# Eight-core attention and block FFN kernel: the float32 to bf16 casts of half of the FFN's second weight move from GpSimd to ScalarE

## The chip, the cores and the metric

The kernel runs on the eight cores of one Trainium2 chip. Each core takes one of the eight batch entries (2048 tokens of 2048 features) and computes its whole output; all weights go to every core, and the cores exchange nothing. The metric is the device time of the slowest core, in microseconds (us). "Before" and "after" are timed as medians of several runs.

## What is computed

The reference, cut to what matters (x is 8 x 2048 x 2048, float32):

```python
xn = layernorm(x)
# attention without a softmax, 16 heads of 128
q, k, v, u = xn @ Wq, xn @ Wk, xn @ Wv, xn @ Wu
q = relu(q) / sqrt(128); k = relu(k) / sqrt(128); u = silu(u)
kv = einsum('bhlk,bhlv->bhkv', k, v)
s  = (rms_norm(einsum('bhlk,bhkv->bhlv', q, kv)) * u) @ Wo
# FFN in 16 blocks of 512 hidden features; each token keeps its 4 best blocks
mask = top4(softmax(xn @ Wr.T + br))          # tokens x 16
h = gelu(xn @ W1.T) * mask                    # tokens x 8192, a mask value per block
g = silu(h @ W2.T)                            # W2.T is 8192 x 2048
out = x + s * g
```

## The kernel before

Five engines each run an instruction list of their own, in order: TensorE (PE), VectorE (DVE), ScalarE (ACT), GpSimd (POOL) and SyncE (SP). They meet only at semaphores that count upward. cT, cV, cS and cG count the finished operations of PE, DVE, ACT and POOL. dS0 to dS3 and dG0 to dG3 count the transfers issued by SP and by POOL, four semaphores each in turn. The helper `dma` makes its engine wait until the transfer issued four before it on the same family has landed. The order of each list is the order in which the Python code appends to it; nothing reorders it afterwards. A wait holds everything behind it on its engine.

The work goes through stages: layer norm, transposes and the router (to about 611 us in the profile), K, V and their product (to 1394 us), the FFN (to 4967 us), then Q, U and attention by head (to 6662 us), and last the output projection with Wo (L621 to L665).

The change is in the FFN. It is done for two halves of 1024 tokens (`Hh`), and in each half for 8 slabs of 1024 hidden features (`slab`), so 16 slabs in all. One slab is:

- Mask rows: four small DMAs `mrow` (L396), four small matmuls (L398), and two casts to `mbc` by ACT (L402).
- GEMM 1, eight steps `jc`: SP loads two halves of a W1 tile (`w1ring`, L411), ACT casts them to bf16 (`w1b`, L414), PE does 32 matmuls of 128x512 into `hps` (L423), ACT applies gelu into `hm` (L427), DVE multiplies by the mask (L431).
- GEMM 2, twice, for the output halves `fh` = 0 and 1 of 1024 features each. First 16 tiles of W2 (128 x 512 float32, 256 KB) are loaded (L445) and cast into the bf16 buffer `w2b[fh]`. Only when all 16 have been cast does PE start 128 matmuls into `yps` (L463), 16 for each of 8 token tiles, and DVE adds each result to `y_acc` in SBUF (L472, or copies it in the first slab, L470).

The 16 W2 tiles pass through `w2ring`, two float32 buffers that both halves share. For `fh` = 0 SP issues the transfers and ACT casts (L450). For `fh` = 1 POOL issues them and POOL itself casts (L453). `w2cast_slot` and `w2cast_slot_g` hold the semaphore values of the last cast by ACT and by POOL from each buffer; the issuing engine waits for both before it overwrites the buffer. The first half's matmuls of PE (from `w2b[0]`) and the second half's loads (into `w2b[1]`) can run side by side.

The same form of ring appears once more, in the output projection: two buffers `woring`, loads by POOL (L633), casts by ACT (L637), 16 tiles of 128 x 512 float32, and PE starts (L651) when all have been cast.

Of the kernel before, what the change touches and what calls it, by code (L numbers as in the profile page):

```python
# [92 lines left out]
def build(nc):  # L93
    es = ExitStack()
    p = Prog(nc, es)
# [21 lines left out]
    cT = p.sem("cT")  # L117
    cV = p.sem("cV")
    cS = p.sem("cS")
    cG = p.sem("cG")  # L120
# [172 lines left out]
    for ncx in range(4):  # L293
        par = ncx % 2
        for i in range(NC):
            rs = (ncx * NC + i) % 4
            p.w("sync", cS, wring_cast[rs])
            dd = p.dma("sync", lambda e, i=i, ncx=ncx, rs=rs: e.dma_start(out=wring[rs][:], in_=wk_d[i * 128:(i + 1) * 128, ncx * 512:(ncx + 1) * 512]), dS)
# [5 lines left out]
        for i in range(NC):  # L304
            rs = (ncx * NC + i) % 4
            p.w("sync", cS, wring_cast[rs])
            dd = p.dma("sync", lambda e, i=i, ncx=ncx, rs=rs: e.dma_start(out=wring[rs][:], in_=wv_d[i * 128:(i + 1) * 128, ncx * 512:(ncx + 1) * 512]), dS)
# [51 lines left out]
    w2b = [p3.enter_context(nc.sbuf_tensor(f"w2b{i}", [128, 8 * 1024], BF16)) for i in range(2)]  # L359
# [14 lines left out]
    w2cast_slot = [0, 0]  # L374
    w2cast_slot_g = [0, 0]
    w2cons_fh = [0, 0]
# [5 lines left out]
    for Hh in range(2):  # L382
        tok0 = Hh * 1024
        for slab in range(8):
            b0 = slab * 2
            if (Hh, slab) != (0, 0):
                p.w("tensor", cS, gelu_done[(Hh, slab - 1, 7) if slab > 0 else (Hh - 1, 7, 7)])
            p.w("tensor", cS, mask_done[NT - 1])
            for bb in range(2):
                b = b0 + bb  # L390
                if bb == 1:
                    p.w("tensor", cS, p.v(cS))
                for gg in range(2):
                    p.w("sync", cS, mask_done[NT - 1])
                    p.w("sync", cT, mrow_guard[0])
                    mrow_dma = p.dma("sync", lambda e, b=b, gg=gg, tok0=tok0: e.dma_start(out=mrow[0:1, :], in_=maskT[b:b + 1, tok0 + gg * 512: tok0 + (gg + 1) * 512]), dS)  # L396
                    p.wd("tensor", mrow_dma)
                    p.e("tensor", lambda e, gg=gg: e.matmul(hps[0][:, gg * 512:(gg + 1) * 512], onesrb[0:1, :], mrow[0:1, :], start=True, stop=True), inc=cT)  # L398
                    mrow_guard[0] = p.v(cT)
                bcmm = p.v(cT)  # L400
                p.w("scalar", cT, bcmm)
                p.e("scalar", lambda e, bb=bb: e.copy(out=mbc[bb][:], in_=hps[0][:, 0:1024]), inc=cS)  # L402
            mbc_done = p.v(cS)
            p.w("tensor", cS, mbc_done)

            for jc in range(8):
                jg = slab * 8 + jc
                sl = jc % 2
                for hf in range(2):
                    p.w("sync", cS, w1cast[hf])  # L410
                    w1dma[hf] = p.dma("sync", lambda e, jg=jg, hf=hf: e.dma_start(out=w1ring[hf][:], in_=w1r_d[jg, :, hf * 1024:(hf + 1) * 1024]), dS)  # L411
                    p.wd("scalar", w1dma[hf])
                    p.w("scalar", cT, w1cons[hf])
                    p.e("scalar", lambda e, hf=hf: e.copy(out=w1b[hf][:], in_=w1ring[hf][:]), inc=cS)  # L414
                    w1cast[hf] = p.v(cS)
                if (Hh * 64 + jg) >= 1:
                    p.w("tensor", cS, gelu_done.get((Hh, slab, jc - 2), gelu_done.get((Hh, slab - 1, jc + 6), 0)))
                for hf in range(2):
                    p.w("tensor", cS, w1cast[hf])
                    for ng in range(2):  # L420
                        for ii in range(8):
                            i = hf * 8 + ii
                            p.e("tensor", lambda e, i=i, ii=ii, ng=ng, sl=sl, hf=hf, tok0=tok0: e.matmul(hps[sl][:, ng * 512:(ng + 1) * 512], w1b[hf][:, ii * 128:(ii + 1) * 128], A[:, i * L + tok0 + ng * 512: i * L + tok0 + (ng + 1) * 512], start=(i == 0), stop=(i == NC - 1)), inc=(cT if (i == NC - 1 and ng == 1) or (ii == 7 and ng == 1) else None))  # L423
                    w1cons[hf] = p.v(cT)
                hmm = p.v(cT)
                p.w("scalar", cT, hmm)
                p.e("scalar", lambda e, jc=jc, sl=sl: e.activation(out=hm[:, jc * 1024:(jc + 1) * 1024], in_=hps[sl][:], func=AF.Gelu), inc=cS)  # L427
                gelu_done[(Hh, slab, jc)] = p.v(cS)
                p.w("vector", cS, gelu_done[(Hh, slab, jc)])
                p.w("vector", cS, mbc_done)  # L430
                p.e("vector", lambda e, jc=jc, bb=jc // 4: e.tensor_tensor(out=hm[:, jc * 1024:(jc + 1) * 1024], in0=hm[:, jc * 1024:(jc + 1) * 1024], in1=mbc[bb][:], op=OP.mult), inc=cV)  # L431
                hmmask_done[(Hh, slab, jc)] = p.v(cV)
            hm_ready = p.v(cV)

            for fh in range(2):
                qeng = "sync" if fh == 0 else "gpsimd"
                qsem = dS if fh == 0 else dG
                ceng = "scalar" if fh == 0 else "gpsimd"
                csem = cS if fh == 0 else cG
                for jc in range(8):  # L440
                    jg = slab * 8 + jc
                    for cc in range(2):
                        p.w(qeng, cS, w2cast_slot[cc])
                        p.w(qeng, cG, w2cast_slot_g[cc])
                        dd = p.dma(qeng, lambda e, jg=jg, fh=fh, cc=cc: e.dma_start(out=w2ring[cc][:], in_=w2t_d[jg * 128:(jg + 1) * 128, fh * 1024 + cc * 512: fh * 1024 + (cc + 1) * 512]), qsem)  # L445
                        p.wd(ceng, dd)
                        if jc == 0 and cc == 0:
                            p.w(ceng, cT, w2cons_fh[fh])
                        if fh == 0:
                            p.e("scalar", lambda e, jc=jc, fh=fh, cc=cc: e.copy(out=w2b[fh][:, jc * 1024 + cc * 512: jc * 1024 + (cc + 1) * 512], in_=w2ring[cc][:]), inc=cS)  # L450
                            w2cast_slot[cc] = p.v(cS)
                        else:
                            p.e("gpsimd", lambda e, jc=jc, fh=fh, cc=cc: e.tensor_copy(w2b[fh][:, jc * 1024 + cc * 512: jc * 1024 + (cc + 1) * 512], w2ring[cc][:]), inc=cG)  # L453
                            w2cast_slot_g[cc] = p.v(cG)
                w2_ready = p.v(csem)
                p.w("tensor", cV, hm_ready)
                p.w("tensor", csem, w2_ready)
                for t8 in range(8):
                    sl = t8 % 2
                    p.w("tensor", cV, yadd_slot[sl])  # L460
                    for jc in range(8):
                        for fg in range(2):
                            p.e("tensor", lambda e, t8=t8, jc=jc, fg=fg, fh=fh, sl=sl: e.matmul(yps[sl][:, fg * 512:(fg + 1) * 512], hm[:, jc * 1024 + t8 * 128: jc * 1024 + (t8 + 1) * 128], w2b[fh][:, jc * 1024 + fg * 512: jc * 1024 + (fg + 1) * 512], start=(jc == 0), stop=(jc == 7)), inc=(cT if (jc == 7 and fg == 1) else None))  # L463
                    ymm = p.v(cT)
                    p.w("vector", cT, ymm)
                    if slab == 0:
                        if Hh == 1:
                            p.w("vector", cS, silu_mark)
                            p.dbar("vector", dG)
                        p.e("vector", lambda e, t8=t8, fh=fh, sl=sl: e.tensor_copy(y_acc[:, t8 * D + fh * 1024: t8 * D + (fh + 1) * 1024], yps[sl][:]), inc=cV)  # L470
                    else:
                        p.e("vector", lambda e, t8=t8, fh=fh, sl=sl: e.tensor_tensor(out=y_acc[:, t8 * D + fh * 1024: t8 * D + (fh + 1) * 1024], in0=y_acc[:, t8 * D + fh * 1024: t8 * D + (fh + 1) * 1024], in1=yps[sl][:], op=OP.add), inc=cV)  # L472
                    yadd_slot[sl] = p.v(cV)
                w2cons_fh[fh] = p.v(cT)
        yfin = p.v(cV)
        for t8 in range(8):
            p.w("scalar", cV, yfin)
            p.e("scalar", lambda e, t8=t8: e.activation(out=y_acc[:, t8 * D:(t8 + 1) * D], in_=y_acc[:, t8 * D:(t8 + 1) * D], func=AF.Silu), inc=cS)
            gdone = p.v(cS)
            p.w("gpsimd", cS, gdone)  # L480
            gst_dma[0] = p.dma("gpsimd", lambda e, t8=t8, tok0=tok0: e.dma_start(out=g_d[tok0 + t8 * 128: tok0 + (t8 + 1) * 128, :], in_=y_acc[:, t8 * D:(t8 + 1) * D]), dG)
        silu_mark = p.v(cS)
# [258 lines left out]
```

How the kernel before makes its waits and increments, by code:

```python
    def dma(self, eng, fn, q):  # L51
        i = self.val[q + "_i"] % self.NSL
        self.val[q + "_i"] += 1
        sub = f"{q}{i}"
        self.w(eng, sub, self.val[sub])
        self.val[sub] += 16
        h = self.sems[sub]
        self.st[eng].append(lambda e, fn=fn, h=h: fn(e).then_inc(h, 16))
        return (sub, self.val[sub])
# [12 lines left out]
    def w(self, eng, sem, v=None):  # L72
        vv = self.val[sem] if v is None else v
        h = self.sems[sem]
        self.st[eng].append(lambda e, h=h, vv=vv: e.wait_ge(h, vv))
# [1 line left out]
    def e(self, eng, fn, inc=None, k=1, dma=False):  # L77
        if not dma and eng in self.SELF:
            own = self.SELF[eng]
            self.w(eng, own, self.val[own])
            inc, k = own, 1
        if inc is not None:
            h = self.sems[inc]
            self.val[inc] += k
            self.st[eng].append(lambda e, fn=fn, h=h, k=k: fn(e).then_inc(h, k))
        else:
            self.st[eng].append(lambda e, fn=fn: fn(e))
```

## Time and profile before

| what | value |
|---|---|
| three timed runs | 7519.0, 7566.81 and 7606.86 us, median 7566.81 |
| the profiled execution | 7322.0 us |
| its slowest core, number 2: first to last instruction | 7320.1 us |
| its other cores | 7207.8 to 7307.4 us |
| PE busy in the span | 3723.1 us, 51% |
| ACT and DVE busy | 1186.6 us (16%) and 1146.8 us (16%) |
| POOL busy | 638.4 us (9%) |
| mean granted TensorE clock, core 2 | 0.766 |

The profiled execution is one execution of the program under the hardware profiler, and its rows are those of its slowest core where no other is named. Times inside it count from the first instruction. PEld is PE's loading of weights, which runs beside the matmuls. The names SPq and POOLq mark transfers that these engines issue, which are not counted as busy time of the engine; in the timeline a row of a transfer shows how long its issue took. The granted clock is a share of TensorE's full speed: 0.50 is 1.2 GHz and 1.00 is 2.4 GHz.

### The profile page before, as it was taken

What the parts mean: (1) busy time and instruction counts of PE and PEld (TensorE: products, weight loads), DVE (VectorE), ACT (ScalarE), POOL (GpSimd) and SP (SyncE); (2) the same over time, 40 slices, a digit from 0 to 9 for tenths busy, and PEclk for the clock granted to TensorE, in tenths of its full rate; (3) what the DMA queues carried; (4) which work ended last, traced back from release to release, by engine and by line L of the source; (5) the groups of instructions that cost most, each with busy time, mean ns of one, the idle gap of its engine ahead of it and who ended that gap; (6) DMA issues with size and microseconds to landing.
All of it is one profiled execution on the core that took longest, in us unless ns stands there. A gap on an engine that the chain in (4) does not pass through costs nothing.

```text
span 7320.1 us, 49442 instructions; the slowest of 8 cores (7207.8 to 7320.1 us)
## 1 busy us (share of the span) xinstructions
PE 3723.1 (51%) x15250; PEld 1514.3 (21%) x15250; DVE 1146.8 (16%) x1750; ACT 1186.6 (16%) x1667; POOL 638.4 (9%) x1003
## 2 busy tenths in 40 slices
PE   2224777855656555655556565555434443443444
PEld 1112322322222222222222222222111111111111
DVE  3331000010101110101101011101222222222000
ACT  2222111111221111221112111112111111110000
POOL 0000000011000111001110011110000000001222
PEclk9999777777878777877778787777656666666777
DMA  1001111122222222232232222222000000002333
GB/s 42 29 24 52 46 46 41 35 69 81 84 79 71 73 73 81 84 108 74 69 81 83 78 72 70 68 90 69 23 23 12 23 23 23 14 20 60 105 101 102
DMA packets 154608, 439.67 MB, mean 60 GB/s; under 512 B 23232, under 2 KB 23232, under 8 KB 150256
## 3 DMA queue, kind: packets, MB, share of 16 engines
q1 hardware_dynamic: 103424, 251.77, 11.5%
q0 software_dynamic: 50928, 184.75, 8.7%
q8 instruction: 128, 2.10, 0.1%
q14 instruction: 128, 1.05, 0.1%
HBM read 402.82 MB, written 33.55 MB: 60 GB/s over the span
## 4 chain that ended last, share of the span: by engine, by line
PE 40%; DMA 29%; ACT 10%; DVE 9%; issue 8%; POOL 4%; ACTq 0%; DVEq 0%; POOLq 0%; SPq 0%
DMA w2ring<-w2t 17%; PE hps L423 14%; PE yps L463 6%; DMA gst<-gscr 4%; PE kp L322 4%; PE qp L538 4%; PE vp L327 3%; PE qp L547 3%; DVE srow L592 3%; POOL w2b L453 2%; ACT w1b L414 2%; ACT hm L427 2%; PE bcp L597 2%; DMA woring<-wo 2%; DMA wring<-wqr 2%
## 5 line engine op out<-in xcount | busy, mean ns | idle before, releaser
L463 PE MATMUL yps<-w2b,hm 128*128 128x512 bf16 x4096 | 957.6, 399 | 1101.8 <-POOL w2b L453 574.1
L423 PE MATMUL hps<-A,w1b 128*128 128x512 bf16 x4096 | 1025.8, 414 | 342.5 <-ACT w1b L414 342.5
L463 PEld LDWEIGHTS yps<-w2b,hm 128*128 128x128 bf16 x4096 | 414.7, 102 | 1644.8 <-issue 1219.0
L423 PEld LDWEIGHTS hps<-A,w1b 128*128 128x128 bf16 x4096 | 420.2, 105 | 948.3 <-issue 583.1
L472 DVE TENSOR_TENSOR y_acc<-y_acc,yps 128x1024 f32<-128x1024 f32 x224 | 273.6, 1221 | 1516.0 <-PE yps L463 1516.0
L651 PE MATMUL sps<-wob,osb 128*128 128x512 bf16 x1024 | 293.0, 452 | 349.3 <-ACT wob L637 201.6
L538 PE MATMUL qp<-A,wqb 128*128 128x512 bf16 x1024 | 257.6, 419 | 372.9 <-ACT wub L525 372.9
L445 POOL DMA_DIRECT2D w2ring<-w2t x256 | 137.4, 537 | 3325.7 <-ACT w2b L450 3310.1
L322 PE MATMUL kp<-wkb,A 128*128 128x512 bf16 x1024 | 283.3, 440 | 147.5 <-ACT wvb L309 147.5
L597 PE MATMUL bcp<-srow,onesrfs 1*128 1x512 f32 x128 | 130.6, 1121 | 405.2 <-DVE srow L592 405.2
L431 DVE TENSOR_TENSOR hm<-hm,mbc 128x1024 bf16<-128x1024 bf16 x128 | 88.6, 692 | 1437.1 <-ACT hm L427 1437.1
L327 PE MATMUL vp<-wvb,A 128*128 128x512 bf16 x1024 | 277.4, 433 | 0.0
L427 ACT ACTIVATE hm<-hps 128x1024 bf16<-128x1024 f32 x128 | 131.0, 1023 | 899.1 <-PE hps L423 899.0
L414 ACT CAST w1b<-w1ring 128x1024 bf16<-128x1024 f32 x256 | 267.5, 1045 | 50.3 <-DMA w1ring<-w1r 27.9
L402 ACT CAST mbc<-hps 128x1024 bf16<-128x1024 f32 x32 | 32.4, 1012 | 1464.9 <-PE hps L398 1464.8
L547 PE MATMUL qp<-A,wub 128*128 128x512 bf16 x1024 | 223.6, 379 | 14.3 <-ACT qtsb L541 14.3
L592 DVE RECIPROCAL srow<-srow 1x512 f32<-1x512 f32 x64 | 213.8, 3341 | 80.1 <-ACT srow L589 80.1
L453 POOL CAST w2b<-w2ring 128x512 bf16<-128x512 f32 x256 | 157.0, 613 | 756.7 <-DMA w2ring<-w2t 756.7
L651 PEld LDWEIGHTS sps<-wob,osb 128*128 128x128 bf16 x1024 | 111.3, 112 | 532.1 <-issue 461.1
L538 PEld LDWEIGHTS qp<-A,wqb 128*128 128x128 bf16 x1024 | 107.1, 106 | 538.5 <-issue 441.3
L450 ACT CAST w2b<-w2ring 128x512 bf16<-128x512 f32 x256 | 158.0, 617 | 346.8 <-DMA w2ring<-w2t 340.9
L603 POOL TENSOR_TENSOR osb<-tmp,utsb 128x512 bf16<-128x512 f32 x64 | 73.6, 1150 | 1305.4 <-DVE tmp L600 1305.4
(93 smaller groups left out, 2434.7 us busy)
## 6 DMA issues: line engine op xcount, KB each, us to landing
w1ring<-w1r SPq DMA_DIRECT2D x256, 512.0 KB, 4.5
w2ring<-w2t SPq DMA_DIRECT2D x256, 256.0 KB, 3.2
w2ring<-w2t POOLq DMA_DIRECT2D x256, 256.0 KB, 3.2
xtile<-x POOLq DMA_DIRECT2D x16, 1024.0 KB, 6.2
wring<-wk SPq DMA_DIRECT2D x64, 256.0 KB, 4.2
wring<-wv SPq DMA_DIRECT2D x64, 256.0 KB, 4.0
gscr<-y_acc POOLq DMA_DIRECT2D x16, 1024.0 KB, 7.7
wring<-wqr POOLq DMA_DIRECT2D x64, 256.0 KB, 3.4
```

What stands on the lines that cost most here:

```text
L322: p.e("tensor", lambda e, i=i, t=t, par=par, sl=sl: e.matmul(kp[sl][:], A[:, i * L + t * 128: i * L + (t + 1) * 128], wkb[par][:, i * 512: ...
L327: p.e("tensor", lambda e, i=i, t=t, par=par, sl=sl: e.matmul(vp[sl][:], A[:, i * L + t * 128: i * L + (t + 1) * 128], wvb[par][:, i * 512: ...
L414: p.e("scalar", lambda e, hf=hf: e.copy(out=w1b[hf][:], in_=w1ring[hf][:]), inc=cS)
L423: p.e("tensor", lambda e, i=i, ii=ii, ng=ng, sl=sl, hf=hf, tok0=tok0: e.matmul(hps[sl][:, ng * 512:(ng + 1) * 512], w1b[hf][:, ii * 128:(i ...
L427: p.e("scalar", lambda e, jc=jc, sl=sl: e.activation(out=hm[:, jc * 1024:(jc + 1) * 1024], in_=hps[sl][:], func=AF.Gelu), inc=cS)
L453: p.e("gpsimd", lambda e, jc=jc, fh=fh, cc=cc: e.tensor_copy(w2b[fh][:, jc * 1024 + cc * 512: jc * 1024 + (cc + 1) * 512], w2ring[cc][:]), ...
L463: p.e("tensor", lambda e, t8=t8, jc=jc, fg=fg, fh=fh, sl=sl: e.matmul(yps[sl][:, fg * 512:(fg + 1) * 512], hm[:, jc * 1024 + t8 * 128: jc ...
L538: p.e("tensor", lambda e, h=h, i=i, ng=ng, par=par, sl=sl: e.matmul(qp[sl][:], wqb[par][:, i * 128:(i + 1) * 128], A[:, i * L + ng * 512:i ...
L547: p.e("tensor", lambda e, h=h, i=i, ng=ng, par=par, sl=sl: e.matmul(qp[sl][:], wub[par][:, i * 128:(i + 1) * 128], A[:, i * L + ng * 512:i ...
L592: p.e("vector", lambda e, ng=ng: e.reciprocal(out=srow[0:1, 0:512], in_=srow2[0:1, 0:512]), inc=cV)
L597: p.e("tensor", lambda e, ng=ng, sl=sl: e.matmul(bcp[sl][:], onesrf[0:1, :], srow[0:1, 0:512], start=True, stop=True), inc=cT)
L651: p.e("tensor", lambda e, i=i, t=t, sl=sl: e.matmul(sps[sl][:], osb[:, i * L + t * 128: i * L + (t + 1) * 128], wob[:, i * 512:(i + 1) * 5 ...
```

## The change

For `fh` = 1 ACT now does the 16 casts that POOL did, with the same `copy` as for `fh` = 0. POOL keeps the issue of the transfers and waits only for ACT's counter. SP's wait for POOL's casts goes, since there are none. Buffers, tiles, matmuls and their order stay the same. Nothing else in the program is touched.

```diff
             for fh in range(2):
                 qeng = "sync" if fh == 0 else "gpsimd"
                 qsem = dS if fh == 0 else dG
-                ceng = "scalar" if fh == 0 else "gpsimd"
-                csem = cS if fh == 0 else cG
                 for jc in range(8):
                     jg = slab * 8 + jc
                     for cc in range(2):
                         p.w(qeng, cS, w2cast_slot[cc])
-                        p.w(qeng, cG, w2cast_slot_g[cc])
                         dd = p.dma(qeng, lambda e, ...: e.dma_start(out=w2ring[cc][:], in_=w2t_d[...]), qsem)
-                        p.wd(ceng, dd)
+                        p.wd("scalar", dd)
                         if jc == 0 and cc == 0:
-                            p.w(ceng, cT, w2cons_fh[fh])
-                        if fh == 0:
-                            p.e("scalar", lambda e, ...: e.copy(out=w2b[fh][...], in_=w2ring[cc][:]), inc=cS)
-                            w2cast_slot[cc] = p.v(cS)
-                        else:
-                            p.e("gpsimd", lambda e, ...: e.tensor_copy(w2b[fh][...], w2ring[cc][:]), inc=cG)
-                            w2cast_slot_g[cc] = p.v(cG)
-                w2_ready = p.v(csem)
+                            p.w("scalar", cT, w2cons_fh[fh])
+                        p.e("scalar", lambda e, ...: e.copy(out=w2b[fh][...], in_=w2ring[cc][:]), inc=cS)
+                        w2cast_slot[cc] = p.v(cS)
+                w2_ready = p.v(cS)
                 p.w("tensor", cV, hm_ready)
-                p.w("tensor", csem, w2_ready)
+                p.w("tensor", cS, w2_ready)
```

On POOL, at the start of the second half (`fh` = 1) of the first slab, this stood in a row before. The digit after w2ring is the buffer, and the brackets give the semaphores waited for:

```order
L445 DMA w2ring0<-w2t 128x512 [waits cS,cG,dG3]
L453 CAST w2b1<-w2ring0 128x512 [waits dG3,cT,cG]
L445 DMA w2ring1<-w2t 128x512 [waits cS,cG,dG0]
L453 CAST w2b1<-w2ring1 128x512 [waits dG0,cG]
L445 DMA w2ring0<-w2t 128x512 [waits cS,cG,dG1]
L453 CAST w2b1<-w2ring0 128x512 [waits dG1,cG]
```

In the same place on POOL stands now:

```order
L442 DMA w2ring0<-w2t 128x512 [waits cS,dG3]
L442 DMA w2ring1<-w2t 128x512 [waits cS,dG0]
L442 DMA w2ring0<-w2t 128x512 [waits cS,dG1]
L442 DMA w2ring1<-w2t 128x512 [waits cS,dG2]
L442 DMA w2ring0<-w2t 128x512 [waits cS,dG3]
L442 DMA w2ring1<-w2t 128x512 [waits cS,dG0]
```

Before, each cast with its wait for the transfer stood between one issue and the next. Now the issues follow each other, and each waits for ACT's counter.

On ACT, at the end of the first half (`fh` = 0) of the same slab, this stood before. The two casts to mbc belong to the next slab:

```order
L450 CAST w2b0<-w2ring0 128x512 [waits dS0,cS]
L450 CAST w2b0<-w2ring1 128x512 [waits dS1,cS]
L450 CAST w2b0<-w2ring0 128x512 [waits dS2,cS]
L450 CAST w2b0<-w2ring1 128x512 [waits dS3,cS]
L402 CAST mbc0<-hps0 128x1024 [waits cT,cS]
L402 CAST mbc1<-hps0 128x1024 [waits cT,cS]
```

On ACT, from the same place on, stands now:

```order
L446 CAST w2b0<-w2ring0 128x512 [waits dS2,cS]
L446 CAST w2b0<-w2ring1 128x512 [waits dS3,cS]
L446 CAST w2b1<-w2ring0 128x512 [waits dG3,cT,cS]
L446 CAST w2b1<-w2ring1 128x512 [waits dG0,cS]
L446 CAST w2b1<-w2ring0 128x512 [waits dG1,cS]
L446 CAST w2b1<-w2ring1 128x512 [waits dG2,cS]
```

Ten casts further on ACT, at the end of the second half and the start of the next slab, stands now:

```order
L446 CAST w2b1<-w2ring1 128x512 [waits dG0,cS]
L446 CAST w2b1<-w2ring0 128x512 [waits dG1,cS]
L446 CAST w2b1<-w2ring1 128x512 [waits dG2,cS]
L402 CAST mbc0<-hps0 128x1024 [waits cT,cS]
L402 CAST mbc1<-hps0 128x1024 [waits cT,cS]
```

The 16 casts into w2b1, each behind its own transfer of POOL, now stand between the first half's last cast and the next slab's first operation on ACT. PE, DVE and SP have the same instructions in the same order.

## Rows read from the trace of the kernel before

**Rows 1.** The page: its head, and the chain that ended last by line

```profile
span 7320.1 us, 49442 instructions; the slowest of 8 cores (7207.8 to 7320.1 us)
...
DMA w2ring<-w2t 17%; PE hps L423 14%; PE yps L463 6%; DMA gst<-gscr 4%; PE kp L322 4%; PE qp L538 4%; PE vp L327 3%; PE qp L547 3%; DVE srow L592 3%; POOL w2b L453 2%; ACT w1b L414 2%; ACT hm L427 2%; PE bcp L597 2%; DMA woring<-wo 2%; DMA wring<-wqr 2%
```

**Rows 2.** Groups by line: busy us, mean ns | idle before, and its releasers

```profile
L463 PE MATMUL yps<-w2b,hm 128*128 128x512 bf16 x4096 | 957.6, 399 | 1101.8 <-POOL w2b L453 574.1 <-ACT w2b L450 527.7
```

**Rows 3.** Timeline of POOL, second half of one slab: start us, us, what

```profile
2411.47 0.54 POOL L445 DMA_DIRECT2D w2ring<-w2t  x1 [154.79 <-ACT w2b L450]
2414.99 0.61 POOL L453 CAST w2b<-w2ring 128x512 bf16<-128x512 f32 x1 [2.98 <-DMA w2ring<-w2t]
...
2444.45 0.61 POOL L453 CAST w2b<-w2ring 128x512 bf16<-128x512 f32 x1 [2.88 <-DMA w2ring<-w2t]
...
2477.44 0.61 POOL L453 CAST w2b<-w2ring 128x512 bf16<-128x512 f32 x1 [2.86 <-DMA w2ring<-w2t]
```

**Rows 4.** Timeline of PE, the same slab and the start of the next

```profile
2412.60 29.68 PE L463 MATMUL yps<-w2b,hm 128*128 128x512 bf16 x128 [32.41 <-ACT w2b L450]
...
2478.31 29.26 PE L463 MATMUL yps<-w2b,hm 128*128 128x512 bf16 x128 [36.03 <-POOL w2b L453]
...
2518.93 8.71 PE L423 MATMUL hps<-A,w1b 128*128 128x512 bf16 x32 [3.94 <-ACT w1b L414]
...
2591.70 7.07 PE L423 MATMUL hps<-A,w1b 128*128 128x512 bf16 x32 [2.45 <-ACT w1b L414]
```

**Rows 5.** Who waited for whom: total us, times, longest

```profile
ACT mbc L402 <- PE hps L398: 1464.8, 31, 103.0
```

**Rows 6.** Timelines of POOL, ACT and PE in the output projection

```profile
6661.85 1.11 POOL L633 DMA_DIRECT2D woring<-wo  x2
6666.61 0.54 POOL L633 DMA_DIRECT2D woring<-wo  x1 [3.64 <-ACT wob L637]
...
6665.38 0.62 ACT L637 CAST wob<-woring 128x512 bf16<-128x512 f32 x1 [11.49 <-DMA woring<-wo]
...
6698.11 0.62 ACT L637 CAST wob<-woring 128x512 bf16<-128x512 f32 x1 [2.43 <-DMA woring<-wo]
...
6827.90 0.62 ACT L637 CAST wob<-woring 128x512 bf16<-128x512 f32 x1 [127.35 <-DMA woring<-wo]
...
6862.03 0.62 ACT L637 CAST wob<-woring 128x512 bf16<-128x512 f32 x1 [3.11 <-DMA woring<-wo]
...
6700.80 9.51 PE L651 MATMUL sps<-wob,osb 128*128 128x512 bf16 x37 [41.11 <-ACT wob L637]
```

**Rows 7.** Timeline of ACT and PE, first half of the next slab

```profile
2600.03 1.32 ACT L450 CAST w2b<-w2ring 128x512 bf16<-128x512 f32 x2
...
2628.99 1.38 ACT L450 CAST w2b<-w2ring 128x512 bf16<-128x512 f32 x2 [2.86 <-DMA w2ring<-w2t]
...
2630.62 29.89 PE L463 MATMUL yps<-w2b,hm 128*128 128x512 bf16 x128 [31.85 <-ACT w2b L450]
```

**Rows 8.** The tile w2ring: landing after issue, us

```profile
DMA to landing us min/median/max: 2.9/3.2/7.7
```

**Rows 9.** The page, costliest groups: DVE's additions to y_acc

```profile
L472 DVE TENSOR_TENSOR y_acc<-y_acc,yps 128x1024 f32<-128x1024 f32 x224 | 273.6, 1221 | 1516.0 <-PE yps L463 1516.0
```

**Rows 10.** Stretches of cores 1, 2 and 4; the third number from the end: granted clock

```profile
700.00:720.00 20.00, 16.76 (x86) 7.55 (x85) 2.07 (x3) 1.19 (x2) 0.00 (x0) 1.00 0.00 0
...
700.00:720.00 20.00, 17.84 (x74) 7.41 (x73) 1.38 (x2) 1.25 (x3) 0.00 (x0) 0.81 0.00 1
...
4580.00:4600.00 20.00, 20.00 (x95) 9.04 (x94) 7.33 (x6) 0.00 (x0) 4.84 (x9) 1.00 0.28 64
```

**Rows 11.** Timeline of PE, first slab of core 2

```profile
1408.61 10.22 PE L423 MATMUL hps<-A,w1b 128*128 128x512 bf16 x32 [3.78 <-ACT w1b L414]
...
1492.85 8.56 PE L423 MATMUL hps<-A,w1b 128*128 128x512 bf16 x32 [2.73 <-ACT w1b L414]
1534.41 35.61 PE L463 MATMUL yps<-w2b,hm 128*128 128x512 bf16 x128 [33.00 <-ACT w2b L450]
```

More of the change, by code:

```diff
@@ L443, in build @@
                         p.w(qeng, cS, w2cast_slot[cc])
-                        p.w(qeng, cG, w2cast_slot_g[cc])
                         dd = p.dma(qeng, lambda e, jg=jg, fh=fh, cc=cc: e.dma_start(out=w2ring[cc][:], in_=w2t_d[jg * 128:(jg + 1) * 128, fh * 1024 + cc * 512: fh * 1024 + (cc + 1) * 512]), qsem)
-                        p.wd(ceng, dd)
+                        p.wd("scalar", dd)
                         if jc == 0 and cc == 0:
-                            p.w(ceng, cT, w2cons_fh[fh])
-                        if fh == 0:
-                            p.e("scalar", lambda e, jc=jc, fh=fh, cc=cc: e.copy(out=w2b[fh][:, jc * 1024 + cc * 512: jc * 1024 + (cc + 1) * 512], in_=w2ring[cc][:]), inc=cS)
-                            w2cast_slot[cc] = p.v(cS)
-                        else:
-                            p.e("gpsimd", lambda e, jc=jc, fh=fh, cc=cc: e.tensor_copy(w2b[fh][:, jc * 1024 + cc * 512: jc * 1024 + (cc + 1) * 512], w2ring[cc][:]), inc=cG)
-                            w2cast_slot_g[cc] = p.v(cG)
-                w2_ready = p.v(csem)
+                            p.w("scalar", cT, w2cons_fh[fh])
+                        p.e("scalar", lambda e, jc=jc, fh=fh, cc=cc: e.copy(out=w2b[fh][:, jc * 1024 + cc * 512: jc * 1024 + (cc + 1) * 512], in_=w2ring[cc][:]), inc=cS)
+                        w2cast_slot[cc] = p.v(cS)
+                w2_ready = p.v(cS)
                 p.w("tensor", cV, hm_ready)
-                p.w("tensor", csem, w2_ready)
+                p.w("tensor", cS, w2_ready)
                 for t8 in range(8):
```

## The prediction

> **What bounds the kernel now.** I read the page first. Its chain of waits, taken by line, is led by the transfers of W2 into w2ring, 17% of the span and more than any matmul line [rows 1]. So GEMM 2 of the FFN waits for its weights. The groups by line give the size: in front of the matmuls of L463 PE stood idle for 1101.8 us, of which 574.1 us ended with POOL's last cast and 527.7 us with ACT's [rows 2]. Each comes once in each of the 16 slabs, so 35.9 us before each second half and 33.0 us before each first half. The change touches the first of the two.
>
> The timeline of POOL shows why it is so long. A tile is issued, lands, is cast, and only then is the next one issued: casts start at 2414.99, 2444.45 (seven later) and 2477.44 (eight later), so every 4.21 us and then every 4.12 us [rows 3]. A ring of two buffers is used as if it had one, because POOL waits for a transfer in the same list in which it would issue the next. Sixteen such steps cost about 66 us. PE's first half runs at the same time and hides 29.7 us of them; the second half starts at 2478.31, which is 65.7 us after the first half's start at 2412.60 [rows 4].
>
> I call this distance from start to start the offset. Averaged, it is PE's half (957.6 us over 32 halves, 29.9 us) and the 35.9 us of waiting: 65.8 us [rows 2].
>
> **The change part by part.** *POOL issues ahead.* The first two issues of a second half now go out as soon as ACT has emptied each buffer, and every later one when ACT has cast the tile two before it. Two transfers are in flight. The trace has the very same form in the output projection: issue by POOL, cast by ACT, two buffers, 16 tiles of 256 KB [rows 6]. There the first issue starts at 6661.85, the second some 0.55 us later (two issues take 1.11 us), so at 6662.4, and PE starts at 6700.80. From the second issue to PE are 38.4 us.
>
> The second buffer comes free with ACT's last cast of the first half. That ends at 2628.99 + 1.38 = 2630.37, and PE starts at 2630.62, 0.25 us later [rows 7]. From the end of a cast on ACT to POOL's next issue are 0.61 us (6665.38 + 0.62 = 6666.00, issue at 6666.61) [rows 6]. So POOL's second issue starts 0.61 - 0.25 = 0.36 us after PE's first half, and the new offset would be 38.4 + 0.36 = 38.8 us.
>
> *DVE beside it.* In the output projection's first load DVE had nothing to do; here it adds into y_acc, eight additions of 1.22 us in a half [rows 9]. Of this the trace shows only the intervals above: 4.21 us with additions, 4.12 us mostly without [rows 3]. I take 0.09 us for each of eight rounds, 0.7 us, and get an offset of 39.5 us.
>
> *Bounds of the offset.* From below: SP's ring goes round faster. Its casts start at 2600.03 and, seven rounds on, at 2628.99, so 4.14 us a round, against (6698.11 - 6665.38) / 7 = 4.68 us for POOL's [rows 6, 7]. Seven rounds at that pace take off 3.8 us, and without DVE's share the offset is 35.0 us. From above: the output projection's second load took 34.1 us for its seven rounds (6827.90 to 6862.03) instead of 32.7 us, so 1.4 us more, 40.9 us [rows 6]. If each of the eight rounds lost a whole addition of DVE, 1.22 us, it would be 38.8 + 9.8 = 48.6 us. I take 39.5 us, nearest to the rows with the same engines and tiles.
>
> *ACT casts 16 tiles more.* 0.62 us each, 9.9 us in a slab, on ACT. They cost nothing: behind ACT's last cast of a first half stands mbc of the next slab, which needs matmuls that PE does after the second half. ACT waits for these 1464.8 us in all, up to 103.0 us at once [rows 5], so between the halves it has nothing else to do. If this cover failed, each slab would lose up to those 9.9 us. POOL's cast took as long (0.61 us), so a round is not shorter or longer by the engine itself.
>
> *SP's removed wait* was for casts of the slab before, done long ago. Worth nothing.
>
> *What is late next.* With an offset of 39.5 us and a half of 29.9 us PE still waits 9.6 us before the second half. Behind the second half nothing can overtake: the next slab's mask rows need PE, and SP's W1 loads are queued behind those rows. So the gain reaches the end in full. The matmuls themselves I leave unchanged. After an idle time of only 3.94 us PE still took 8.71 us for 32 matmuls and otherwise 7.07 us [rows 4], so the slow start at the lower clock stays after 9.6 us too; if it vanished, 1.6 us a slab more would be won.
>
> *The sum.* 65.8 - 39.5 = 26.3 us a slab, by 16 slabs 421 us. The profiled execution took 7322 us (span 7320.1 us [rows 1]) and would take 6901 us. The median of the timed runs is 7566.81 us, 245 us above it. What they spend it on the trace cannot say, most likely slower matmuls. The gain does not depend on that, since it is a difference of two loading times, both longer than PE's half: even where that half took 35.6 us [rows 11] the new offset of 39.5 us is longer. So 7567 - 421 = 7146 us.
>
> **Rivals.** *The clock gives part back.* In the K and V stage cores 1 and 2 ran matmuls almost without a pause, core 1 with a granted clock of 1.00 and core 2 with 0.81; in the FFN core 4 ran a dense stretch at 1.00 [rows 10]. Core 2 still had slow matmuls in its first slab: GEMM 1 from 1408.61 to 1501.41, 92.8 us, and a half of 35.61 us [rows 11]; later GEMM 1 took from 2518.93 to 2598.77, 79.8 us [rows 4]. The change puts PE's halves closer together. If that made 0.81 hold in all slabs, each would cost 13.0 us more in GEMM 1 and 5.7 us in the second half; the first half's 5.7 us would vanish in the wait that is left. 18.7 by 16 is 299 us, the net gain 122 us, and the time 7445 us; with half the slabs it would be 7295 us. Against it: the wait of 33 us before each first half stays, and dense stretches of the FFN ran at 1.00.
>
> The Trainium skill, "TensorE: Matmul & The Clock Gate", section "Seeing it yourself", says that a peak-current limit takes a whole die to 13/16 of the clock when three of its cores run dense matmuls. The trace agrees with the level (0.81) but not with the whole die, since cores 1 and 2 of one die differed in the same stretch. By the rule alone the price would be the full one above.
>
> *DVE holds up POOL's issues.* If each round waited for one addition, the offset of 48.6 us would leave 17.2 us a slab, 275 us, and 7292 us. Against it: seven intervals among DVE's additions were only 0.09 us longer than eight mostly clear of them [rows 3].
>
> The Trainium skill, "SBUF — State Buffer", section "🔬 SBUF: two separate sides", says that POOL cannot write a transfer's descriptors while VectorE holds the port they share, in a two-port mode. Whether the additions into y_acc are such an operation the trace doesn't say; the intervals speak against it.
>
> *Nothing changes.* If something else kept ACT or POOL from running ahead, such as POOL's wait for the transfer four before, the offset would stay at 65.8 us and the time at 7567 us. Against it: with two in flight the one four before has landed when the buffer is free, and the output projection has the same wait.
>
> *Slower.* Two transfers in flight from eight cores at once could slow each other. The point from which this decides is a round of 65.8 / 8 = 8.2 us for two tiles. The slowest landing seen for w2ring is 7.7 us, against 3.2 us usually [rows 8]; if every one took that, a round would be 7.7 + 0.62 + 0.61 + some 0.1 = 9.0 us and the offset 72 us, 6.4 us a slab more than before, 103 us, and 7670 us. Against it: SP's ring, also with two in flight on all cores, turns in 4.14 us [rows 7].
>
> **How the numbers follow.** The forecast has a chance of 0.80, the clock 0.12 (full or in part), DVE 0.03, no change 0.03, slower 0.02. The forecast's own range goes from an offset of 35.0 us (493 us gained, 7074 us) to 40.9 us (398 us, 7169 us); the timed runs before lay up to 48 us from their median. Down to 7050 us and up, into the clock's partial cases, to 7300 us. About what a measurement of this kernel can tell from no change is 1%, some 76 us: the forecast, DVE and the clock at its full price of 7445 us lie beyond it. Faster by over 1%: 0.95; within 1%: 0.03; slower: 0.02.
>
> **What would show it.** Right: on POOL, issues in pairs about 4.7 us apart from pair to pair, and on ACT 32 casts in a row in each slab; PE's wait before second halves down from 574.1 us to about 150 us, now ended by ACT; the wait before first halves near 528 us as before; L463 near 958 us. The profile's span would be near 6900 us. Wrong: a granted clock of 0.81 in FFN stretches, with L463's and L423's mean duration clearly up, would be the clock; pairs 6 us apart only while DVE adds would be DVE; landings well over 4 us in pairs would be contention; ACT's casts to mbc or w1b starting late would mean that the cover failed.

## The result, and the profile after

The changed kernel takes 6897.5 us, the median of ten runs (6794.3 to 7172.7). The kernel before, timed beside it in ten runs that include the three quoted above, takes 7356.5 us (7234.5 to 7606.9). The ratio is 0.939, with a 95% interval of 0.936 to 0.943: 6% faster, and each of the ten runs after is shorter than each of the ten before. To read these numbers one has to know that in some executions the cores of one die have a lower granted clock and take some per cent longer (in one of the kernel before, cores 4 to 7 had a mean of 0.72 to 0.73 and took 7509 to 7540 us, while cores 0 to 3 had 0.78 and took 7199 to 7268 us), and that the ratio leaves such executions out while the medians don't.

The forecast was 421 us less, 7146 us. The gain is right (6.1% of the 7234.5 us that the kernel before takes at best is 439 us; the two lowest times are 440 us apart). The time is not: it lies under the range of 7050 to 7300 us.

The profiled execution of the changed kernel took 6955.1 us, and its slowest core, number 4, ran part of it at the lower clock (mean 0.766 over its span). Core 2 did not (0.799), and it is also the core whose rows stand above. So here are rows of core 2. First its groups by line, then its waits (total us, times, longest):

```profile
core 2 of [0, 1, 2, 3, 4, 5, 6, 7], span 6780.8 us
L423 PE MATMUL hps<-A,w1b 128*128 128x512 bf16 x4096 | 1013.7, 411 | 342.1 <-ACT w1b L414 342.1
L456 PE MATMUL yps<-w2b,hm 128*128 128x512 bf16 x4096 | 950.9, 397 | 672.2 <-ACT w2b L446 672.2
...
L446 ACT CAST w2b<-w2ring 128x512 bf16<-128x512 f32 x512 | 316.1, 617 | 809.3 <-DMA w2ring<-w2t 803.9 <-ACT w2b L446 0.4
```

```profile
PE yps L456 <- ACT w2b L446: 672.2, 32, 34.4
ACT mbc L402 <- PE hps L398: 533.5, 31, 33.6
```

PE's idle time before the matmuls into yps fell from 1101.8 us [rows 2] to 672.2 us, by 429.6 us. The matmuls are as long as they were (950.9 against 957.6 us), and ACT still has 533.5 us of waiting for the mask matmuls, where it had 1464.8 us [rows 5]. Only 158 us of the difference (16 slabs of 9.9 us) are the further casts themselves; the rest went into ACT's waits for the transfers between them (803.9 us in all, 340.9 us on the page before) and into shorter slabs. All 32 waits of PE now end with ACT. Which of the two kinds shrank is seen in one slab. PE:

```profile
2017.80 30.65 PE L456 MATMUL yps<-w2b,hm 128*128 128x512 bf16 x128 [33.04 <-ACT w2b L446]
2055.14 5.10 PE L456 MATMUL yps<-w2b,hm 128*128 128x512 bf16 x17 [6.70 <-ACT w2b L446]
```

The wait before the first half is as before; the one before the second half is 6.70 us where it was 36.03 us [rows 4]. (The second row is cut off by the end of the stretch shown.) The offset from start to start is 37.3 us here. Over the 16 slabs of core 2 it was 66.0 us on average before and is 39.0 us now; the waits before second halves sum to 148 us now, against 574 us, and those before first halves to 525 us, against 528 us.

POOL in the same slab, and ACT's casts of the same tiles:

```profile
2018.16 0.54 POOL L442 DMA_DIRECT2D w2ring<-w2t  x1 [0.55 <-ACT w2b L446]
2021.67 0.54 POOL L442 DMA_DIRECT2D w2ring<-w2t  x1 [2.97 <-ACT w2b L446]
2022.88 0.54 POOL L442 DMA_DIRECT2D w2ring<-w2t  x1 [0.68 <-ACT w2b L446]
2026.28 0.54 POOL L442 DMA_DIRECT2D w2ring<-w2t  x1 [2.86 <-ACT w2b L446]
...
2050.91 0.54 POOL L442 DMA_DIRECT2D w2ring<-w2t  x1 [1.27 <-ACT w2b L446]
```

```profile
2020.43 0.62 ACT L446 CAST w2b<-w2ring 128x512 bf16<-128x512 f32 x1 [2.89 <-DMA w2ring<-w2t]
2021.65 0.62 ACT L446 CAST w2b<-w2ring 128x512 bf16<-128x512 f32 x1 [0.60 <-DMA w2ring<-w2t]
2025.05 0.62 ACT L446 CAST w2b<-w2ring 128x512 bf16<-128x512 f32 x1 [2.78 <-DMA w2ring<-w2t]
...
2054.27 0.62 ACT L446 CAST w2b<-w2ring 128x512 bf16<-128x512 f32 x1 [1.19 <-DMA w2ring<-w2t]
```

A buffer is issued again every 4.6 to 4.7 us (2021.67 to 2026.28, 2018.16 to 2022.88), and in that time two tiles go through; from cast to cast a round of two is 4.75 us on average over the 16 slabs of core 2. Before, one tile took 4.1 to 4.2 us [rows 3]. The last cast ends at 2054.89 and PE starts 0.25 us later.

### The profile page after: what moved, and what is told of

Its sections match the earlier page's. It is cut to its first block, busy times and chain, and to the rows that moved or that the text cites. A ratio compares the mean times of both kernels' runs of the same rounds, so it can differ in the third digit from the quotient of the medians.

```text
span 6953.0 us, 48930 instructions; the slowest of 8 cores (6764.7 to 6953.0 us)
## 1 busy us (share of the span) xinstructions
PE 3850.2 (55%) x15250; PEld 1543.5 (22%) x15250; DVE 1147.0 (16%) x1750; ACT 1344.6 (19%) x1923; POOL 481.4 (7%) x747
## 4 chain that ended last, share of the span: by engine, by line
PE 43%; DMA 24%; ACT 11%; DVE 9%; issue 9%; POOL 1%; ACTq 1%; DVEq 0%; POOLq 0%; SPq 0%
PE hps L423 16%; DMA w2ring<-w2t 12%; PE yps L456 7%; DMA gst<-gscr 4%; PE kp L322 4%; PE qp L531 4%; PE vp L327 4%; PE qp L540 3%; DVE srow L585 3%; ACT w2b L446 2%; ACT w1b L414 2%; ACT hm L427 2%; PE bcp L590 2%; DMA woring<-wo 2%; DMA wring<-wur 2%
## 5 line engine op out<-in xcount | busy, mean ns | idle before, releaser
L456 PE MATMUL yps<-w2b,hm 128*128 128x512 bf16 x4096 | 1020.8, 418 | 622.2 <-ACT w2b L446 622.2
L423 PE MATMUL hps<-A,w1b 128*128 128x512 bf16 x4096 | 1096.6, 435 | 343.2 <-ACT w1b L414 343.2
L456 PEld LDWEIGHTS yps<-w2b,hm 128*128 128x128 bf16 x4096 | 428.9, 105 | 1214.3 <-issue 946.2
L423 PEld LDWEIGHTS hps<-A,w1b 128*128 128x128 bf16 x4096 | 436.6, 109 | 1002.9 <-issue 771.4
L446 ACT CAST w2b<-w2ring 128x512 bf16<-128x512 f32 x512 | 316.1, 617 | 803.7 <-DMA w2ring<-w2t 798.0
L560 DVE COPY attnsb<-ap 128x512 f32<-128x512 f32 x64 | 44.2, 691 | 867.2 <-PE ap L557 860.4
L322 PEld LDWEIGHTS kp<-wkb,A 128*128 128x128 bf16 x1024 | 108.2, 108 | 277.3 <-issue 262.2
```

The lines of the kernel that those rows point to most:

```text
L322: p.e("tensor", lambda e, i=i, t=t, par=par, sl=sl: e.matmul(kp[sl][:], A[:, i * L + t * 128: i * L + (t + 1) * 128], wkb[par][:, i * 512: ...
```

## The experiments

Seven kernels ran, each beside the kernel before on the same chip. The offsets and sums of waits below are worked out from the starts and idle times of PE's matmuls into yps on core 2, over 16 slabs. A quotient is that of the two lowest times. "..." marks what is left out of a piece of code, and the comments in the code are this document's.

**1. POOL casts, but issues ahead.** This is the kernel before with the order on POOL changed, so that two transfers are in flight without any cast moving to ACT.

```diff
+                ahead = [w2load(0), w2load(1)]      # transfer of tile k, with its waits
+                for k in range(16):
+                    p.wd(ceng, ahead[k])
...
+                    if k < 14:
+                        ahead.append(w2load(k + 2))
```

> The kernel before, with POOL still casting the second half's tiles itself, but with each transfer issued ahead: the first two before the first cast, and tile k+2 right behind the cast of tile k. Theory (the gain comes from two transfers in flight, whoever casts): a round of two tiles takes 3.45 + 0.61 + 0.04 = 4.1 us, the offset between the starts of PE's two halves falls from 65.8 to about 34.5 us, shorter than the changed kernel's since no handoff from ACT to POOL is left. 31 us a slab, about 500 us: ratio to before 0.93. Rival (the gain comes from POOL being rid of the casts): the offset stays near 65 us, ratio 1.00.

The profiled execution took 6899.4 us; the lowest time of the kernel before beside it was 7278.2 us, a quotient of 0.948. The offset was 43.1 us and the waits before second halves 212 us. So most of the gain (22.9 of 27.0 us a slab) comes without touching ACT, and the rival (the engine that casts) is out. The size was missed: an offset of 34.5 us and a ratio of 0.93 were expected. One stretch of POOL shows why:

```profile
2226.85 0.61 POOL L456 CAST w2b<-w2ring 128x512 bf16<-128x512 f32 x1 [2.64 <-DMA w2ring<-w2t]
2228.08 0.54 POOL L445 DMA_DIRECT2D w2ring<-w2t  x1 [0.62 <-POOL w2b L456]
2228.61 0.62 POOL L456 CAST w2b<-w2ring 128x512 bf16<-128x512 f32 x1
2229.85 0.54 POOL L445 DMA_DIRECT2D w2ring<-w2t  x1 [0.62 <-POOL w2b L456]
2231.75 0.61 POOL L456 CAST w2b<-w2ring 128x512 bf16<-128x512 f32 x1 [1.36 <-DMA w2ring<-w2t]
```

Between the end of its own cast and the next issue POOL stood for 0.62 us, released by that cast. I had put 0.04 us there, read from the kernel before, where the issue after a cast filled the other buffer and had nothing fresh to wait for:

```profile
2415.64 0.54 POOL L445 DMA_DIRECT2D w2ring<-w2t  x1
```

This issue follows the cast that ends at 2414.99 + 0.61 = 2415.60 [rows 3]. A wait on the result of the instruction just done costs POOL as much as one on ACT's (0.61 us [rows 6]). And since cast, wait and issue stand in one list, the second buffer's cast is held back by the first buffer's issue. A round took 4.90 us here (2226.85 to 2231.75), 0.80 us more than expected: 0.58 us of it is this wait, 0.22 us the time from issue to cast (3.67 us instead of 3.45 us). Over the 16 slabs a round is 5.3 us on average, where the changed kernel has 4.75 us. So that ACT casts is worth something after all: 43.1 - 39.0 = 4.1 us a slab on core 2, and 2.2 us on core 5 (41.5 against 39.2 us).

**2. SP issues both halves.** The changed kernel with POOL out of the loads.

```diff
-                qeng = "sync" if fh == 0 else "gpsimd"
-                qsem = dS if fh == 0 else dG
+                qeng = "sync"
+                qsem = dS
```

> The changed kernel, but SP issues the second half's transfers too, as it does for the first half. Theory: the rounds take SP's 4.14 us instead of POOL's 4.68 us, the offset is about 34.5 us, PE waits 4 to 5 us before a second half instead of 9 us, and some 70 us go: ratio to before 0.93. Rival (POOL's longer rounds come from the transfers themselves or from DVE's additions beside them): same rounds of 4.7 us, ratio 0.94.

Ratio 0.924 (0.916 to 0.931); the offset 34.9 us, the waits before second halves 83 us. The theory holds: the longer round belongs to POOL's way of issuing, not to the memory, the ring or DVE. It gives the lower bound of 35.0 us that I had put under the offset.

**3. ACT casts, one transfer in flight.**

```diff
-                        p.w(qeng, cS, w2cast_slot[cc])
+                        p.w(qeng, cS, w2cast_slot[cc] if fh == 0 else max(w2cast_slot))
```

> The changed kernel (ACT casts), but with one transfer of the second half in flight at a time: POOL waits for the last cast of either buffer before each issue. Theory: a tile costs 0.61 + 3.45 + 0.62 = 4.7 us, the offset is about 75 us, 9 us a slab more than before: slower than before by about 150 us, ratio 1.02. Rival (the engine that casts matters, not the order): faster than before, ratio 0.94 to 0.97.

Ratio 1.020 (1.015 to 1.025): slower than before, as forecast. POOL's issues and ACT's casts, in alternation:

```profile
2204.56 0.54 POOL L442 DMA_DIRECT2D w2ring<-w2t  x1 [4.28 <-ACT w2b L446]
2209.11 0.54 POOL L442 DMA_DIRECT2D w2ring<-w2t  x1 [4.01 <-ACT w2b L446]
```

```profile
2203.33 0.62 ACT L446 CAST w2b<-w2ring 128x512 bf16<-128x512 f32 x1 [4.20 <-DMA w2ring<-w2t]
2207.88 0.62 ACT L446 CAST w2b<-w2ring 128x512 bf16<-128x512 f32 x1 [3.93 <-DMA w2ring<-w2t]
```

A cast ends at 2203.95, the issue starts 0.61 us later, and the next cast 3.32 us after that: 4.5 us for one tile, the offset 77.3 us. With the casts on ACT in both, one transfer in flight or two is the difference between 2% slower and 6% faster than before.

**4. All W2 tiles in GEMM 1.** POOL issues and ACT casts four tiles in each of the eight steps, between the casts of W1 and the gelu.

```diff
+                for k in range(4 * jc, 4 * jc + 4):
+                    fh, kk = k // 16, k % 16
...
+                    p.w("gpsimd", cS, w2cast_slot[cc])
+                    dd = p.dma("gpsimd", lambda e, ...: e.dma_start(out=w2ring[cc][:], in_=w2t_d[...]), dG)
+                    p.wd("scalar", dd)
...
+                    p.e("scalar", lambda e, ...: e.copy(out=w2b[fh][...], in_=w2ring[cc][:]), inc=cS)
```

> All 32 W2 tiles of a slab are loaded by POOL and cast by ACT during GEMM 1, four per step, between the casts of W1 and the gelu. Theory (ACT has 6 to 8 us free in each step, so both waits of PE before its halves go): 31 us before the first half and 9 us before the second go, less some 2 us a slab for steps in which ACT is late: about 600 us less than the changed kernel, ratio to before 0.86. Rival (the clock): PE then hardly pauses, the granted clock is 0.81 through the FFN as in the K and V stage, each slab pays 24 us of it back: ratio 0.91, with L423 and the matmuls into yps near 500 ns on average.

Ratio 0.866 (0.862 to 0.871), with 6356.8 us in the profiled execution. The page's costliest groups:

```profile
L433 PE MATMUL hps<-A,w1b 128*128 128x512 bf16 x4013 | 1085.4, 434 | 492.9 <-ACT w1b L414 486.3
L454 PE MATMUL yps<-w2b,hm 128*128 128x512 bf16 x4014 | 900.6, 385 | 50.2 <-DVE hm L441 45.8
```

PE no longer waits for W2: 50.2 us before all 32 halves, where it was 1101.8 us. The matmuls have not slowed to 500 ns, so the clock did not take it back. They did shift: GEMM 1's (L433) now take 434 ns on average, 60 us more in all than on the page before (L423, 414 ns), and those into yps 385 ns instead of 399 ns, 57 us less. What is late is ACT in GEMM 1: the idle time before L433 went from 342.5 us on the page before to 492.9 us. The landing of a W2 tile took 4.4 us in the median, where it was 3.2 us [rows 8].

**5. DVE's additions cut down.** Only 8 of 1024 columns are added beside POOL's issues, so that half of the sum is left out.

```diff
+                        w = 1024 if fh == 1 else 8
```

> The changed kernel, but in the first output half (beside which POOL issues the second half's transfers) DVE adds only 8 of the 1024 columns of each result into y_acc, so that half of the output is left incomplete. Theory (DVE's additions hardly hold up POOL's issues): the offset stays within 1 us of the changed kernel's 39.0 us, and PE's wait before second halves near 148 us. Rival (each addition holds POOL up): rounds of two tiles fall by up to 1.2 us, the offset to 30 to 35 us, the wait to under 80 us.

The offset stayed at 39.0 us, the waits before second halves at 145 us, the profiled execution at 6799.7 us. The additions don't hold POOL up. The 0.7 us that I had given them is not there either.

**6. Four buffers.** The ring of W2 takes in the two W1 buffers, which nobody uses between the last step of GEMM 1 and the next slab.

```diff
+    w2r = [w2ring[0][:], w2ring[1][:], w1ring[0][:, 0:512], w1ring[1][:, 0:512]]
...
+                        rr = (jc % 2) * 2 + cc
+                        p.w(qeng, cS, w2cast_slot[rr])
+                        if rr >= 2:
+                            p.w(qeng, cS, w1cast[rr - 2])
```

> The changed kernel with a ring of four W2 buffers for both halves; the two more are the W1 buffers, which are free at that time. Theory (what is paid is the latency of each transfer, not its bytes): four tiles turn in about 5 to 5.5 us, the offset falls under PE's half of 29.9 us so that the wait before second halves goes, and the wait before first halves falls from 33 to about 19 us: some 370 us less than the changed kernel, ratio to before 0.89. Rival (two tiles in 4.2 us are already what the transfers can carry beside seven other cores): four in flight land twice as late, nothing is won, ratio 0.94.

6413.5 us in the profiled execution, with 7223.2 us as the lowest of the kernel before beside it: a quotient of 0.888. PE on core 2:

```profile
2105.60 58.19 PE L461 MATMUL yps<-w2b,hm 128*128 128x512 bf16 x251 [20.21 <-ACT w2b L451]
```

Both halves now run as one, 58 us long, and the only wait is the one before the first, about 20 us. On the slowest core it sums to 338.2 us in 16 slabs, 21.1 us each (19 us had been expected). A transfer lands in 3.8 to 4.3 us in the median, by issuing engine and buffer, instead of 3.2 to 3.3 us, so four in flight carry far more than two. What PE had waited for was latency, not bytes.

**7. Both joined.** The first half's tiles in GEMM 1, two per step; the second half's beside PE's first half, with four buffers.

```diff
+                for cc in range(2):        # in each step jc of GEMM 1
+                    p.w("gpsimd", cS, w2cast_slot[cc])
+                    dd = p.dma("gpsimd", lambda e, ...: e.dma_start(out=w2r[cc], in_=w2t_d[...]), dG)
+                    p.wd("scalar", dd)
...
-                for jc in range(8):
+                for jc in range(8 if fh == 1 else 0):
```

> The two experiments joined: the first half's 16 W2 tiles are loaded and cast during GEMM 1 (two per step, ring of two), the second half's 16 beside PE's first half with a ring of four. Theory: neither half waits for weights any more, and with two tiles a step instead of four ACT is no longer late, so that GEMM 1's idle time is back from 493 us to about 345 us: 130 to 150 us less than with all tiles in GEMM 1, some 6210 us, ratio to before 0.855. Rival (the clock gives it back once PE hardly pauses): the granted clock in the FFN falls to 0.81 and the time is no better than 6360 us, ratio 0.87 or more.

6139.9 us, the lowest time and the profiled one, against 7278.8 us as the lowest of the kernel before beside it: a quotient of 0.844. The page's groups for the two GEMMs:

```profile
L433 PE MATMUL hps<-A,w1b 128*128 128x512 bf16 x4096 | 1017.1, 412 | 344.1 <-ACT w1b L416 344.1
L469 PE MATMUL yps<-w2b,hm 128*128 128x512 bf16 x4096 | 898.4, 382 | 39.5 <-DVE hm L441 39.5
```

GEMM 1's wait is back at 344.1 us, as the theory said to within a microsecond, and W2 costs PE nothing. The time is 70 us under the 6210 us that were expected: with the idle time (492.9 to 344.1 us, 148.8 us less) the matmuls of L433 also got shorter (1085.4 to 1017.1 us, 68.3 us less), which the expectation left out. Together that is 217 us, the difference between the two profiled executions (6356.8 and 6139.9 us). Why these matmuls are slower where ACT is late was not tried. Three stretches of the FFN on core 2 show the clock (the third number from the end):

```profile
1900.00:2300.00 400.00, 312.17 (x1313) 131.81 (x1312) 58.13 (x58) 132.68 (x162) 45.61 (x85) 0.92 0.40 118
2300.00:2900.00 600.00, 463.28 (x1968) 197.20 (x1967) 98.33 (x93) 191.17 (x225) 67.06 (x125) 0.90 0.40 119
2900.00:3600.00 700.00, 565.76 (x2421) 241.56 (x2419) 121.99 (x115) 212.22 (x267) 80.45 (x150) 0.93 0.39 110
```

The mean granted clock is 0.90 to 0.93. In the kernel before, the same core had this from 2300 us on, and this in one wait before a second half:

```profile
2300.00:2900.00 600.00, 340.89 (x1415) 142.95 (x1412) 65.47 (x64) 106.43 (x123) 50.39 (x88) 0.80 0.27 81
...
2442.30:2478.30 36.00, 0.00 (x0) 0.02 (x1) 1.22 (x1) 0.00 (x0) 9.81 (x17) 0.57 0.24 66
```

PE is busy for 463 us of 600 instead of 341 us, and the mean went up, because the long waits, with a mean of 0.57 in the one shown, close to the 0.50 of 1.2 GHz, are gone. The rest did not get faster: without its five waits for W2 (171 us, mean 0.55) the stretch of the kernel before stands at 0.90 too. (Both are means of the clock over those times in the trace of core 2.)

## Why the prediction was right, and where it was wrong

**The step that failed** is the last line of the sum: "So 7567 - 421 = 7146 us". The 421 us were measured; the 7567 us were not what the kernel before takes. Ten runs give it a median of 7356.5 us, and the three that I had turned out to be its three slowest; the other seven lie between 7234.5 and 7470.2 us. The profile had hinted at it: it took 7322 us. I wrote that the median stood 245 us above it and then took the median without asking which was the typical one. What the three runs spent the 245 us on, no measurement of their cores shows; the execution of 7199 to 7540 us by core quoted with the result fits the "slower matmuls" of the prediction. The range was built on the same base, with 48 us for its scatter, and so missed too.

Against the profiled execution the same sum gives 6901 us, and the measured median is 6897.5 us. That they agree within 4 us is luck. The profiled execution of the kernel before was itself 88 us above the lowest time, mostly because its cores 2 and 3 ran the K and V stage at the lower clock (below), and the median after is the middle of a gap in which no run lies: five runs took 6794 to 6825 us and five 6970 to 7173 us. The sound comparison is between the lowest times: 7234.5 - 421 = 6813.5 us, measured 6794.3 us.

**The offset before** was put at 65.8 us; the starts give 66.0 us. Right.

**The offset after**, 39.5 us, was taken from the output projection, the nearest rows with the same engines, buffers and tiles. Measured: 39.0 us. Of the parts, the 38.8 us without DVE was the better number. DVE's 0.7 us came from a difference of 0.09 us between seven and eight intervals, and experiment 5 shows that it was scatter: without the additions the offset is the same 39.0 us. For the same reason the rival "DVE holds up POOL's issues" is out.

**The gain in a slab** was put at 26.3 us. Measured on core 2: 27.0 us, and by 16 slabs 432 us. Its first and last halves before and after say the same of the whole FFN. The rows of the last slab before, and of the first and last slab after:

```profile
4937.08 30.36 PE L463 MATMUL yps<-w2b,hm 128*128 128x512 bf16 x128 [33.59 <-POOL w2b L453]
```

```profile
1432.62 29.70 PE L456 MATMUL yps<-w2b,hm 128*128 128x512 bf16 x128 [32.03 <-ACT w2b L446]
...
4394.23 30.27 PE L456 MATMUL yps<-w2b,hm 128*128 128x512 bf16 x128 [7.02 <-ACT w2b L446]
```

From the first half of the first slab to the second half of the last: 3402.7 us before (from 1534.41 [rows 11]), 2961.6 us after, 441 us less. Core 2's span fell by 539 us, more than that. Of the rest, 102 us lie ahead of the first half of GEMM 2, which it reaches at 1432.6 us instead of 1534.4 us; what follows the last half took 4 us longer. The change has no part in the 102 us. In the profile before, this core ran the K and V stage and its first slab at a lower clock [rows 10, 11], and in the one after it did not (mean from 700 to 1380 us: 0.77 before, 0.90 after). That is a second reason to take the ratio and not two spans.

**ACT's 16 further casts cost nothing.** Right: before the mask casts it still waits 533.5 us.

**Two transfers in flight, not the engine that casts.** Right in the main part (experiments 1 and 3). The sentence "a round is not shorter or longer by the engine itself" was wrong by 4.1 us a slab on core 2 and 2.2 us on core 5, as experiment 1 showed: an engine that casts and issues in one list pays the wait for its own cast and holds up the other buffer.

**The wait that is left.** 9.6 us a slab and about 150 us in all were forecast; 148 us were measured. That it is the issuing engine's round which sets it was shown by experiment 2 (SP: 83 us).

**The clock.** The rival with a chance of 0.12 did not come to pass: L423 is at 411 ns on core 2 in the changed kernel (414 ns on the page before), and a kernel with PE far busier ran at a mean of 0.90 to 0.93 in its profiled execution (experiment 7). What decides when a group of cores falls to 0.81 was not tried and stays open. It does fall at times: in the profiled execution of the changed kernel core 4 had L456 at 418 ns, while core 2 had 397 ns. The rival's full price, 299 us, would leave a gain of 122 us; the medians of all ten runs, which leave nothing out, differ by 459 us. The rule of the Trainium skill, "TensorE: Matmul & The Clock Gate", section "Seeing it yourself", is that three cores with dense matmuls take their whole die to 13/16. The trace does not agree: from 700 to 720 us of the profile before, PE was busy for 16.6 to 17.9 of the 20 us on all eight cores, and cores 2 and 3 had 0.81, the other six 1.00.

**Nothing changes, or slower through contention.** Out: transfers of POOL land in 3.3 us in the median with two in flight, and with four in 3.9 to 4.0 us (experiment 6).

## What to carry to other kernels

A ring of two buffers is only double buffering if the issue of the next transfer does not stand behind the wait for the present one in the same engine's list; look for an engine that alternates transfer, cast, transfer, cast at a constant interval. Then ask what the consumer waits for: here it was the latency of single transfers (3.3 us each, by 16), so more in flight, or loading them in a stage in which the casting engine has time, gave another 5 to 10% beyond the change itself. And when a gain is turned into a time, see first whether the profiled execution and the few timed runs agree; where they are 3% apart, the base is the largest uncertainty of the forecast and belongs in the range.

## What was not expected of the hardware

- A wait of POOL for the instruction it has just finished costs 0.62 us, as much as a wait for another engine (0.61 us). Where the wait is for something long done, the next issue follows 0.04 us after a cast (experiment 1 and the kernel before).
- With the same buffers, tiles and casting engine, SP's ring of two needs 4.1 us less per 16 tiles than POOL's on core 2 (offset 34.9 against 39.0 us) and 5.3 us less on core 5 (33.9 against 39.2 us).
- From two to four transfers in flight on each of eight cores the median landing time rose only from 3.2 or 3.3 us to between 3.8 and 4.3 us, while 512 KB in flight on each core became 1 MB.
- Busier matmuls did not bring the lower clock in the profiled execution of experiment 7: with PE busy for 463 of 600 us the mean granted clock was 0.90. The 0.80 of the kernel before, with 341 us, is an average over long waits at 0.55 and the rest at 0.90.
